# A two-layer graph network on one core: gathers released by the sums of the group that used the buffer, own terms inside the edge stages, setup and node stages rewritten without loops

## The chip, the core and the metric

The kernel runs on one core of one Trainium2 chip. A core has five engines with queues of their own: PE (TensorE, matrix products), DVE (VectorE), ACT (ScalarE), POOL (GpSimd) and SP (SyncE, which here only starts DMAs). They work side by side and wait for one another through semaphores. The metric is the time of one execution of the program in microseconds, taken on the device.

## What is computed

6250 nodes with 160 floats each (64 scalars and 32 vectors of three components), 200000 edges sorted by destination, and two layers. Each takes a message per edge, sums the messages by destination, mixes them and adds them to the node, and normalizes the row. Layer 0, shortened:

```python
xs, xv = node_input[:, :64], node_input[:, 64:].reshape(n, 32, 3)
s_s, s_v = xs * attr @ Ws_sc_a + ..., ...            # own terms, attributes a and c
x1s, x1v = l1a_s + l1c_s, l1a_v + l1c_v              # what the edges gather
weight = silu(edge_length_embedded @ W_fc1) @ W_fc2  # 192 weights per edge
gs, gv = x1s[edge_src], x1v[edge_src]
mid0a = w0 * gs * e_s
mid0b = w3 * (einsum('euc,ec->eu', gv, e_v) / sqrt(3))
mid1a = w1[:, :, None] * gs[:, :, None] * e_v[:, None, :]
mid1b = w2[:, :, None] * gv * e_s[:, :, None]
agg = segment_sum(edge_feat, edge_dst) / sqrt(16)
o = ((agg @ Ws_l2) @ Ws_l3) ...
x = layernorm(x + C_S * s + C_X * o)
```

Layer 1 is alike, with 224 weights per edge from 64 features, a fifth message (`w5 * cross(ev, e1) / sqrt(2)`), and at the end `silu` of 64 scalars and a `sigmoid` gate on the 32 vectors: `x = layernorm(x + gated)`.

## The kernel before

Nodes are padded to 6400, in 50 tiles of 128. Edges are cut into G = 392 groups of 512 (four tiles of 128 edges), four groups to a body, 98 bodies. There are five stages, each a block of its own with a barrier of all engines between: `setup_phase`, `edge_phase` of layer 0, `layer0_nodes_phase`, `edge_phase` of layer 1, `layer1_nodes_phase`.

**Setup** computes for each tile of nodes the row that edges will gather, and stores it to `table0` in DRAM. PE does two products a tile (L243 with 96 rows of x, L244 with 64), ACT scales one half (L221), DVE adds the other (L277), and SP stores. Ahead of the tiles PE multiplies the l2 and l3 matrices (L233, 16 products), and DVE finds each group's lowest and highest destination (L252 converts to float, L254, L255) and later a running sum of how many windows a group needs beyond the first (the scan, L298, L299). POOL loads x and clears `sums` (L206), the array of 128 features by nodes in SBUF in which both layers add up.

**Edge stage.** For each group:

- POOL gathers 512 rows from `table{L}`, in four instructions of 128 rows (L415). It has four row buffers, one per group of a body. A group's gathers wait for `index_in` and for `msg_done` of the group that had the buffer, so for the end of DVE's messages.
- PE computes the hidden layer (L450), ACT its silu (L431), PE the edge weights (L461).
- DVE builds `match` (one where the edge's destination is column n of a window of 40 nodes, L537), ACT scales it with the components of the edge attribute (L438), 12 or 16 small instructions per group.
- DVE multiplies rows and weights to messages: L618, L624, L626, in layer 1 also L608, L609, L623, L629 for the cross product. The last one signals `msg_done`.
- PE sums (L470): products of messages (as weights, 64 or 32 columns wide, each width going to a part of PE's columns) with `match` (40 or 3 × 40 columns). Over a group they accumulate in one PSUM bank. Every float32 product appears in the trace as two records: 56 per group in layer 0, 72 in layer 1.
- DVE adds the window to `sums` (L557).

PE's order, written out, is hidden layer of group g, edge weights of g−1, sums of g−2. SP loads indices, edge inputs and attributes two groups at a time, each load waiting for the reader of the buffer.

**Node stages** run tile by tile in loops of ten: ACT copies a piece of `sums` into a staging tile (L741, L875), PE multiplies own terms (L768, L769) and aggregates (L771 to L773; layer 1 L908 to L911), DVE combines, takes mean and variance and normalizes; in layer 0 PE transposes the new row (L779, L780) and multiplies it for the next layer (L786 to L788), and SP stores the new x, the new table and the own terms of layer 1. POOL loads, and at the end of the stage clears `sums` (L717).

## Time and profile before

| what | us |
|---|---|
| median of 3 runs | 4455.87 (4447.93 to 4457.54) |
| the profiled execution | 4453.04 |
| its span, from the first to the last instruction | 4451.0 |
| PE busy | 4044.4 (91%) |
| POOL busy | 3054.0 (69%) |
| ACT busy | 2961.5 (67%) |
| DVE busy | 2847.8 (64%) |

The mean granted PE clock over the span is 0.976 of full speed. A row of the timeline reads: start and length in us, engine, line of the kernel, operation, what it writes <- what it reads, shape, how many of the like in a row; in brackets how long the engine had been idle before it and what ended that. "PEld" is PE's loading of weights, which overlaps its products. "issue" is idle time in which the engine waited for nothing that the profile shows. A share of busy time doesn't tell what bounds a stage: that is read from the stage's own rows, in the section behind the diff.

### The profile page before, as it was taken

Reading aid. Unit: us, or ns where it says so; the run is one execution under the profiler, and the core shown is the slowest. Engines: PE = TensorE matmul, PEld = TensorE weight load, DVE = VectorE, ACT = ScalarE, POOL = GpSimd, SP = SyncE. Lnnn points to the kernel's source line nnn. Section 1 sums busy time; section 2 is a strip of 40 time slices with the busy share of each in tenths; the row PEclk is TensorE's granted clock in tenths of the full one; section 3 lists DMA queues with packets and bytes.
Section 4 is the critical chain, followed back from the end, with each engine's and each line's share of the span. In section 5 each row is a group of like instructions: output and inputs, shape, how many; then the busy total and the mean of one; then the engine's idle time right before and its main releaser. Section 6 shows DMA issues by size and latency. Waiting matters only on the chain. (4 is left out here: it accounts for less than half of the span.)

```text
span 4451.0 us, 166762 instructions
## 1 busy us (share of the span) xinstructions
PE 4044.4 (91%) x58000; PEld 3053.2 (69%) x58001; DVE 2847.8 (64%) x7746; ACT 2961.5 (67%) x12216; POOL 3054.0 (69%) x3215
## 2 busy tenths in 40 slices
PE   7888888888888888888979999999999999999987
PEld 4677777777777777776756766666666666666666
DVE  4544444444444444444667888888888888888878
ACT  1566666666666666665337877777777777777753
POOL 2577777777777777776017777777777777777751
PEclk9999999999999999999889999999999999999995
DMA  4222222222222222223334444444444444444433
GB/s 107 71 72 73 72 72 72 72 73 73 72 73 73 72 72 72 72 73 68 104 98 129 121 120 120 122 121 120 121 121 121 121 121 121 122 121 121 121 100 94
DMA packets 356348, 430.11 MB, mean 97 GB/s; under 512 B 203298, under 2 KB 248648, under 8 KB 356112
## 3 DMA queue, kind: packets, MB, share of 16 engines
q0 software_dynamic: 156288, 329.79, 27.4%
q1 hardware_dynamic: 199618, 98.11, 8.2%
q10 hardware_dynamic: 400, 1.68, 0.1%
q8 instruction: 23, 0.38, 0.0%
q14 instruction: 19, 0.16, 0.0%
HBM read 405.56 MB, written 23.74 MB: 96 GB/s over the span
## 5 line engine op out<-in xcount | busy, mean ns | idle before, releaser
L415 POOL DMA_INDIRECT e_rows<-scratch_table,e_index x3136 | 2967.3, 946 | 1010.5 <-issue 926.2
L438 ACT ACTIVATE e_match<-e_match,e_attr 128x40 f32<-128x40 f32 x10976 | 2480.9, 315 | 176.3 <-DMA e_attr<-in_edge_attr 172.1
L470 PEld LDWEIGHTS e_sum<-e_match,e_msg 128*64 128x64 f32 (+1 forms) x50176 | 1714.0, 125 | 698.3 <-DVE e_msg L629 244.3
L470 PE MATMUL e_sum<-e_match,e_msg 128*64 128x40 f32 (+2 forms) x50176 | 1846.2, 223 | 247.5 <-DVE e_msg L626 194.6
L461 PE MATMUL e_w<-k_fc,e_hidden 100*128 100x192 f32 (+1 forms) x4704 | 1275.2, 407 | 0.0
L618 DVE TENSOR_TENSOR e_msg<-e_w,e_rows 128x512 f32<-128x512 f32 x784 | 537.8, 686 | 1008.1 <-DMA e_rows<-scratch_table,e_index 980.0
L461 PEld LDWEIGHTS e_w<-k_fc,e_hidden 100*128 100x128 f32 (+1 forms) x4704 | 833.0, 190 | 385.3 <-issue 364.8
L431 ACT ACTIVATE e_hidden<-e_h 100x512 f32<-100x512 f32 (+1 forms) x784 | 384.4, 490 | 925.9 <-PE e_h L450 921.2
L450 PE MATMUL e_h<-e_inputs,k_fc 128*100 128x512 f32 (+1 forms) x1568 | 708.6, 534 | 57.9 <-DMA e_inputs<-in_inputs 27.0
L608 DVE TENSOR_TENSOR e_misc<-e_misc,e_rows 128x384 f32<-128x384 f32 x392 | 221.8, 566 | 354.2 <-DMA e_rows<-scratch_table,e_index 354.1
L624 DVE TENSOR_TENSOR e_msg<-e_w,e_rows 128x384 f32<-128x384 f32 x784 | 428.1, 546 | 0.0
L626 DVE TENSOR_TENSOR e_msg<-e_w,e_rows 128x384 f32<-128x384 f32 x784 | 428.0, 546 | 0.0
L450 PEld LDWEIGHTS e_h<-e_inputs,k_fc 128*100 128x100 f32 (+1 forms) x1568 | 216.0, 177 | 115.8 <-issue 54.9
L537 DVE TENSOR_TENSOR e_match<-e_misc,e_dst_rel 128x160 f32<-128x160 f32 x788 | 248.0, 315 | 13.3 <-DMA e_dst_rel<-scratch_dst_rel 11.1
L557 DVE TENSOR_TENSOR sums<-sums,e_sum 128x120 f32 (+1 forms) x784 | 226.3, 289 | 18.5 <-PE e_sum L470 16.9
L609 DVE TENSOR_TENSOR e_cross_b<-e_misc,e_rows 128x384 f32<-128x384 f32 x392 | 214.3, 547 | 0.0
L623 DVE TENSOR_TENSOR e_msg<-e_misc,e_cross_b 128x384 f32<-128x384 f32 x392 | 214.1, 546 | 0.0
L629 DVE TENSOR_TENSOR e_msg<-e_w,e_msg 128x384 f32<-128x384 f32 x392 | 213.4, 544 | 0.0
L601 DVE TENSOR_TENSOR e_match<-e_misc,e_match 128x160 f32<-128x160 f32 x392 | 123.4, 315 | 0.3 <-DVE e_match L537 0.2
L712 POOL DMA_DIRECT2D m_xv<-in_xT_v x10 | 5.4, 540 | 153.9 <-DVE m_y L805 142.5
L588 DVE COPY e_misc<-e_attr 128x48 f32<-128x48 f32 x392 | 79.8, 203 | 18.3 <-issue 5.9
L741 ACT ACTIVATE m_staged<-sums 128x384 f32 (+1 forms) x50 | 26.0, 522 | 97.1 <-PE m_agg L773 80.8
(122 smaller groups left out, 1454.0 us busy)
## 6 DMA issues: line engine op xcount, KB each, us to landing
e_rows<-scratch_table,e_index POOLq DMA_INDIRECT x3136
e_inputs<-in_inputs SPq DMA_DIRECT2D x196, 256.0 KB
e_attr<-in_edge_attr SPq DMA_DIRECT2D x392, 24.0 KB, 1.7
e_inputs<-in_inputs SPq DMA_DIRECT2D x196, 40.0 KB
e_index<-in_src SPq DMA_DIRECT2D x392, 4.0 KB
scratch_self<-m_h SPq DMA_DIRECT2D x10, 480.0 KB, 4.5
f_self<-scratch_self POOLq DMA_DIRECT2D x10, 480.0 KB, 5.0
m_xrow<-in_x POOLq DMA_DIRECT2D x10, 400.0 KB, 5.0
```

What stands on the lines that cost most here:

```text
L415: pool.indirect_dma_start(out=rows[j][:, t, :], out_offset=None, in_=table_dram, in_offset=bass.IndirectOffsetOnAxis(ap=index[q][:, c:c + ...
L431: nc.scalar.activation(hidden[j % 2][:, :], ps_h[0:layer.hid, 0:layer.group_cols], ACT.Silu, scale=layer.silu_scale).then_inc(silu_done, 1)
L438: last = nc.scalar.activation(match[j][:, t, c, :], match[j][:, t, 4, :], ACT.Copy, scale=attr[q][:, e0 + t, e:e + 1])
L450: nc.tensor.matmul(ps_h[0:layer.hid, 0:n], w[f"fc1_{L}"][:, :], inputs[j // 2][:, (j % 2) * n:(j % 2) * n + n], start=True, stop=True).the ...
L461: last = nc.tensor.matmul(ps_w[j % 2][:, c0:c0 + n], hidden[j % 2][:, u * P:(u + 1) * P], w[f"fc2_{L}"][:, :], start=True, stop=True)
L470: return nc.tensor.matmul(out[rows, c0:c0 + n, :], m[:, t, f:f + rows.stop - rows.start], m5[:, t, which:which + n, :], start=(first and t ...
L537: return nc.vector.tensor_tensor(into[:, :, 4, :], iota_t, rel_of(g).unsqueeze(2).broadcast_to([P, TPG, WIN]), ALU.is_equal)
L557: nc.vector.tensor_tensor(at, at, window, ALU.add).then_inc(added, 1)
L608: nc.vector.tensor_tensor(comps(cross_a), e3(3), comps(r[:, :, 96:192]), ALU.mult)
L618: nc.vector.tensor_tensor(m[:, :, 0:128].rearrange("p t (k n) -> p t k n", k=2), wt[:, :, 0:128].rearrange("p t (k n) -> p t k n", k=2), r ...
L624: nc.vector.tensor_tensor(comps(m[:, :, 128:224]), w_v(128), comps(r[:, :, 64:160]), ALU.mult)
L626: last = nc.vector.tensor_tensor(comps(m[:, :, 224:320]), w_v(160), comps(r[:, :, 64:160]), ALU.mult)
```

## The change

Nothing of what is computed changes, but nearly every stage is rewritten.

**Gathers.** A row buffer is now released by `sum_done`, the end of PE's sums for the group that used it, not by `msg_done`. The first four groups of a stage wait for nothing: the index buffers are four instead of two, are kept over stages, and are first filled in setup. POOL's loop covers two bodies per turn. A gathered row has 160 floats in both layers. On POOL's queue, in layer 0's loop, before (a row per run of like instructions; `DMA` is a gather):

```order
L415 DMA e0_rows0<-scratch_table0,e0_index0 128x160 [waits e0_msg_done0,e0_index_in0,e0_prepared]
L415 DMA e0_rows0<-scratch_table0,e0_index0 128x160 x3
L415 DMA e0_rows1<-scratch_table0,e0_index0 128x160 [waits e0_msg_done1,e0_index_in0,e0_prepared]
L415 DMA e0_rows1<-scratch_table0,e0_index0 128x160 x3
L415 DMA e0_rows2<-scratch_table0,e0_index1 128x160 [waits e0_msg_done2,e0_index_in1,e0_prepared]
```

and now, at the start of the stage and the head of the loop:

```order
L542 DMA e0_rows3<-scratch_table0,k_index3 128x160 x3
L549 UNCONDITIONAL_BRANCH
L549 ISA
L553 ISA
L542 DMA e0_rows0<-scratch_table0,k_index0 128x160 [waits e0_sum_done,e0_index_in0,e0_prepared]
L542 DMA e0_rows0<-scratch_table0,k_index0 128x160 x3
L542 DMA e0_rows1<-scratch_table0,k_index0 128x160 [waits e0_sum_done,e0_index_in0,e0_prepared]
```

The runs of four gathers stay; the semaphore that each run waits for is another one, and the wait compares it with a sum held in registers.

**Sums.** All products are 32 columns wide, dealt to the four quarters of PE's columns in turn: ten per tile in layer 0 and twelve in layer 1, so 80 and 96 records per group. Layer 1's cross product is no longer formed by DVE; its two halves are two more messages with their own `match` component, the second with negated weights. PE's queue, layer 0, one group's sums before:

```order
L470 MATMUL e_sum<-e_match,e_msg 64x120 [waits e0_scaled,e0_msg_done0]
L470 MATMUL e_sum<-e_match,e_msg 64x40 x2
L470 MATMUL e_sum<-e_match,e_msg 64x120
L470 MATMUL e_sum<-e_match,e_msg 64x40 x2
L470 MATMUL e_sum<-e_match,e_msg 64x120
L470 MATMUL e_sum<-e_match,e_msg 64x40 x2
L470 MATMUL e_sum<-e_match,e_msg 64x120
L470 MATMUL e_sum<-e_match,e_msg 64x40 x2
L470 MATMUL e_sum<-e_match,e_msg 32x40 x16
```

and now, in a group that also carries own terms (`e_xb` is a tile of x, transposed):

```order
L607 MATMUL e_sum<-e_match,e_msg 32x120
L607 MATMUL e_sum<-e_match,e_msg 32x40 x8
L607 MATMUL e_sum<-e_match,e_msg 32x120 x2
L607 MATMUL e_sum<-e_match,e_msg 32x40 x8
L607 MATMUL e_sum<-e_match,e_msg 32x120 x2
L607 MATMUL e_sum<-e_match,e_msg 32x40 x8
L607 MATMUL e_sum<-e_match,e_msg 32x120 x2
L607 MATMUL e_sum<-e_match,e_msg 32x40 x8
L637 MATMUL e_sum<-k_node_v,e_xb 128x2x96 [waits e0_base_in]
L638 MATMUL e_sum<-k_node_s,e_xb 128x2x64
```

The 64-wide products are gone, the two products of own terms stand behind the group's sums and ahead of the signal `sum_done`.

**Own terms** of tile i are computed in body i of the edge stage, i < 50, two PE products and two DVE operations, into `nodes`, which stays in SBUF (`base`, `node_terms`); SP loads the tile and in layer 1 stores the scaled own terms.

**Layer 1's edge weights** take four products of 64 rows and 256 columns instead of two of 128 rows and 480.

**Setup.** Tiles are written out one by one. x comes in large pieces on SP's and ACT's queues; all products have 128 rows (DVE clears the 32 rows that pad x). Ten products of the identity with itself stand in front, the l matrices' fold (four products) behind tile 44, the groups' minimum and maximum on DVE at tiles 13 and 17 without the conversion, and the scan is replaced by one PE product. POOL clears `sums` in seven pieces and ACT does an eighth.

**Node stages** are written out tile by tile. PE reads `sums` itself as weights, with no staging copy. In layer 0 the row isn't normalized before it is transposed; the next layer's weights are centred in setup, and the scaling by 1/deviation is applied behind. PE's queue in the middle of layer 0's stage, before:

```order
L768 MATMUL m_self<-k_node_v,m_xv 128x2x96 [waits m_y_ready,m_stage_done]
L769 MATMUL m_self<-k_node_s,m_xs 128x2x64
L771 MATMUL m_agg<-k_out,m_staged 128x320
L772 MATMUL m_agg<-k_out,m_staged 128x2x64
L773 MATMUL m_agg<-k_out,m_staged 128x2x96
L779 MATMUL m_tr<-k_ident,m_x_0 96x128 [waits m_trs_copied,m_x1_ready]
L780 MATMUL m_tr<-k_ident,m_x_0 64x128
L786 MATMUL m_next<-k_node_v,m_x1Tv 128x2x96 [waits m_h1_ready,m_trs_copied]
L787 MATMUL m_next<-k_node_s,m_x1Ts 128x64
L788 MATMUL m_next<-k_node_s,m_x1Ts 128x96
```

and now:

```order
L933 MATMUL m_agg<-k_out,sums 128x2x64 [waits m_y_done]
L934 MATMUL m_agg<-k_out,sums 128x2x64
L935 MATMUL m_agg<-k_out,sums 128x2x32
L937 MATMUL m_agg<-k_out,sums 128x2x64
L943 MATMUL m_tr<-k_ident,nodes 128x128 [waits m_tr_copied,m_momented]
L944 MATMUL m_tr<-k_ident,nodes 128x128
L950 MATMUL m_next<-k_node_v,m_yT 128x96 [waits m_h_ready,m_tr_copied]
L951 MATMUL m_next<-k_node_s,m_yT 128x64
```

Own terms have left the tile, and half of the next layer's product (its own terms) too. POOL clears `sums` tile by tile behind the products (L865). In layer 1's stage the own terms come in four loads, ACT normalizes in six batches, and 11 stores follow.

The core of the diff:

```diff
@@ edge_phase, POOL @@
-            def gather(count, j):
-                q = j // 2
-                pool.wait_ge(prepared, 1)
-                pool.wait_ge(index_in[q], count)
-                pool.wait_ge(msg_done[j], count)
+            def gather(count, summed, parity, j):
+                k = 2 * parity + j // 2
+                if not isinstance(count, int):
+                    pool.wait_ge(prepared, 1)
+                    pool.wait_ge(index_in[k], count)
+                    pool.wait_ge(sum_done, summed[GPB * parity + j])
+                elif parity:
+                    pool.wait_ge(sum_done, j + 1)
...
-            for j in range(GPB):
-                gather(16, j)
-            with pool.Fori(32, 16 * BODIES + 16, 16) as count:
-                for j in range(GPB):
-                    gather(count, j)
+            for parity in range(2):
+                for j in range(GPB):
+                    gather(0, None, parity, j)
+            with pool.Fori(1, BODIES // 2) as pair:
+                count = 32 * pair
+                summed = [2 * GPB * pair + (o - GPB + 1) for o in range(2 * GPB)]
+                for value in (count, *summed):
+                    pool.compute_val(value)
+                for parity in range(2):
+                    for j in range(GPB):
+                        gather(count, summed, parity, j)
@@ edge_phase, PE @@
-                    c0, n = u * layer.tiles_per_product * WPITCH, w[f"fc2_{L}"].shape[1]
-                    last = nc.tensor.matmul(ps_w[j % 2][:, c0:c0 + n], hidden[j % 2][:, u * P:(u + 1) * P], w[f"fc2_{L}"][:, :],
-                                            start=True, stop=True)
+                    for h in range(layer.tiles_per_product):
+                        c0, k = (u + 2 * h) * WPITCH, fc2.shape[0] // layer.tiles_per_product
+                        last = nc.tensor.matmul(ps_w[j % 2][:, c0:c0 + n], hidden[j % 2][k * h:k * h + k, u * P:(u + 1) * P],
+                                                fc2[k * h:k * h + k, :], start=True, stop=True)
...
-            def window_sums(j, m5):
+            def tile_sums(out, m, m5, opens, closes):
+
+                def product(g, c0, f, which, n=1, first=False, end=False):
+                    return nc.tensor.matmul(out[32 * g:32 * g + 32, c0:c0 + n, :], m[:, f:f + 32],
+                                            m5[:, which:which + n, :], start=first and opens, stop=end and closes)
+                product(0, 0, 64, 0, n=3, first=True)
+                product(1, 0, 96, 0, n=3, first=True)
+                product(2, 0, 128, 3, first=True)
+                product(3, 3, 224, 0, first=True)
+                if L == 0:
+                    product(2, 1, 160, 3)
+                    product(3, 3, 256, 1)
+                    product(0, 3, 0, 3, end=True)
+                    product(1, 3, 32, 3, end=True)
+                    product(2, 2, 192, 3, end=True)
+                    return product(3, 3, 288, 2, end=True)
...
+                if with_base:
+                    last = base(i)
+                last.then_inc(sum_done, 1)
```

## Rows read from the trace of the kernel before

**Rows 1.** Page of the profile: the span, and the gathers' line with its idle time.
```profile
span 4451.0 us, 166762 instructions
L415 POOL DMA_INDIRECT e_rows<-scratch_table,e_index x3136 | 2967.3, 946 | 1010.5 <-issue 926.2
```

**Rows 2.** Timeline: start us, us, engine, line, what, [idle before it <-releaser]. Gathers of both layers.
```profile
138.02 1.02 POOL L415 DMA_INDIRECT e_rows<-scratch_table,e_index  x1 [31.21 <-DVE e_misc L528]
...
993.74 0.95 POOL L415 DMA_INDIRECT e_rows<-scratch_table,e_index  x1 [0.30 <-issue]
...
1002.49 0.95 POOL L415 DMA_INDIRECT e_rows<-scratch_table,e_index  x1 [0.30 <-issue]
1003.75 0.95 POOL L415 DMA_INDIRECT e_rows<-scratch_table,e_index  x1 [0.30 <-issue]
...
2098.14 0.95 POOL L415 DMA_INDIRECT e_rows<-scratch_table,e_index  x1 [0.31 <-issue]
...
2338.41 1.01 POOL L415 DMA_INDIRECT e_rows<-scratch_table,e_index  x1 [24.40 <-DMA e_index<-in_src]
...
4298.60 0.95 POOL L415 DMA_INDIRECT e_rows<-scratch_table,e_index  x1 [0.30 <-issue]
```

**Rows 3.** Timeline of PE: one group of layer 0.
```profile
999.78 1.47 PE L461 MATMUL e_w<-k_fc,e_hidden 100*128 100x192 f32 x8
1001.71 2.12 PE L470 MATMUL e_sum<-e_match,e_msg 128*64 128x120 f32 x56 [0.46 <-DVE e_msg L626]
1003.75 1.10 PE L450 MATMUL e_h<-e_inputs,k_fc 128*100 128x512 f32 x2
```

**Rows 4.** One line's instructions: L470 on PE in two stretches of that group.
```profile
L470 PE MATMUL e_sum<-e_match,e_msg x24: 229/229/317, 1001.7 to 1002.6; 128*64 128x40 f32 x16, 128*64 128x120 f32 x8
L470 PE MATMUL e_sum<-e_match,e_msg x34: 202/202/229, 1002.5 to 1003.6; 128*32 128x40 f32 x32, 128*64 128x40 f32 x2
```

**Rows 5.** Timeline of layer 1: one group on PE; the last group's sums and addition.
```profile
3001.72 0.70 PE L450 MATMUL e_h<-e_inputs,k_fc 128*128 128x256 f32 x2
3002.26 1.77 PE L461 MATMUL e_w<-k_fc,e_hidden 128*128 128x480 f32 x4
...
4306.88 0.54 DVE L629 TENSOR_TENSOR e_msg<-e_w,e_msg 128x384 f32<-128x384 f32 x1
...
4307.48 4.10 PE L470 MATMUL e_sum<-e_match,e_msg 128*64 128x120 f32 x72 [4.07 <-DVE e_msg L629]
4311.78 0.32 DVE L557 TENSOR_TENSOR sums<-sums,e_sum 128x160 f32 x1 [4.13 <-PE e_sum L470]
```

**Rows 6.** Timeline of setup.
```profile
4.34 21.59 POOL L206 MEMSET sums<- 128x25760 f32 x1
7.34 19.68 DVE L252 TENSOR_SCALAR dst_by_group_f<-dst_by_group 98x2048 f32<-98x2048 int32 x1 [7.20 <-DMA dst_by_group<-in_dst_by_group]
...
20.00 7.09 PE L233 MATMUL ps_out<-s_l 96*128 96x32 f32 x32 [20.00 <-DMA s_l<-in_l]
...
41.96 1.01 PE L243 MATMUL s_psn<-k_node_v,s_xv 96*128 96x192 f32 x2 [11.74 <-DVE h L277]
42.89 0.50 PEld L244 LDWEIGHTS s_psn<-k_node_s,s_xs 64*128 64x128 f32 x2 [0.44 <-issue]
...
43.62 0.50 PEld L243 LDWEIGHTS s_psn<-k_node_v,s_xv 96*128 96x128 f32 x2 [0.22 <-issue]
...
122.39 0.38 DVE L277 SCALAR_TENSOR_TENSOR h<-s_psn,k_attr,part_a 128x160 f32<-128x160 f32 x1 [1.28 <-ACT part_a L221]
```

**Rows 7.** Timeline: the first stage of nodes, what precedes and ends it.
```profile
2109.21 0.28 DVE L557 TENSOR_TENSOR sums<-sums,e_sum 128x120 f32 x1 [3.75 <-PE e_sum L470]
...
2331.89 0.50 SPq L732 DMA_DIRECT2D scratch_self<-m_h  x1
```

**Rows 8.** Table of stretches: busy us (x) of PE, PEld, DVE, ACT, POOL, PEclk, DMA share, GB/s.
```profile
2120.00:2290.00 170.00, 163.78 (x767) 120.69 (x767) 115.41 (x401) 64.03 (x211) 15.96 (x24) 0.88 0.37 102
4320.00:4433.00 113.00, 95.16 (x384) 85.77 (x384) 94.49 (x447) 44.67 (x147) 13.92 (x16) 0.59 0.22 66
```

1274 lines of the change are left out of this document (715 added, 559 removed).

## The prediction, made before the changed kernel was run

> **What bounds the kernel now.** First the page: POOL's gathers are 3136 instructions, 2967.3 us busy, and the idle time before them is 926.2 us of "issue", time in which POOL waited for nothing that the profile shows [rows 1]. 926.2 over 3136 gathers is 0.30 us each, and the timeline has that 0.30 before every gather of the steady state: starts are 0.95 + 0.30 = 1.25 us apart [rows 2]. Then the ends of the two rows of gathers: layer 0 runs from 138.02 to 2098.14 + 0.95 = 2099.09, layer 1 from 2338.41 to 4298.60 + 0.95 = 4299.55 [rows 2]. Both are 1961.1 us for 1568 gathers, 1.251 each, though a row has 160 floats in the one and 224 in the other. So in 3922 of the 4451 us POOL issues gathers without a stop, and neither the release of a row buffer nor the bytes set the pace. Last what lies around them: setup 138.0; from layer 0's last gather to its last addition 2109.49 − 2099.09 = 10.4 [rows 2, 7]; the nodes' stage from there to layer 1's first gather 228.9; the same tail in layer 1 4312.10 − 4299.55 = 12.5 [rows 2, 5]; the last stage 4451.0 − 4312.1 = 138.9 [rows 1, 5]. These 528.8 us are all that the change can shorten, unless it changes the pace of POOL.
>
> **The edge stages.** The same 3136 gathers are issued, each still 128 rows. The release moves from the messages to the sums of the group that used the buffer. With four buffers a group's gathers start 4 × 5.0 = 20 us before the buffer is wanted again. The group whose sums run from 1001.71 to 1003.75 [rows 3] had its first gather at 993.74 [rows 2], the eighth before 1003.75: 10.0 us, so the new wait has some 10 us to spare. The worst cases are the last groups, with PE at slow clock: first gather 3.75 us before the last, sums over at 2109.21 and 4311.78 [rows 5, 7], that is 14.8 and 16.9 us, still under 20. The messages are queued on DVE and the sums on PE, in group order in both versions; who waits if the sums were late is POOL alone, with all later gathers behind it. I count the release at nothing, and what hides it is this slack. The register arithmetic of the new wait runs on POOL's queue at 49 loop heads where 97 were; the old heads cost nothing visible [rows 1, 2], and I take nothing.
>
> PE must stay under 5.0 us per group. In layer 0 it runs the hidden layer from 1003.75 to 1004.69 (the next start), 0.94; edge weights, eight records of 192 columns, about 1.30; sums 2.04 (1001.71 to 1003.75) [rows 3], together 4.3. The sums go from 56 records to 80 with 32-column weights, in layer 1 from 72 to 96. The 32-wide part of the old sums shows what such records cost: 32 of them start between 1002.8 and 1003.6, 26 ns each [rows 4] (the row's window also catches two of the 64-wide kind), though 24 of the 32 go to one group of PE's columns, so groups run beside each other. At 26 ns the new sums take 80 × 0.026 = 2.1 and 96 × 0.026 = 2.5 us. PE in layer 0: 0.94 + 1.30 + 2.1 = 4.3. In layer 1: hidden 0.54, edge weights 1.70 before (four records of 480 columns [rows 5]), less after (eight of 256), 2.5: at most 4.7. Below 5.0 both times. Own terms add two products every fourth group in the first 50 bodies, 4 records of at most 192 columns at 0.16 = 0.65 us, or 0.16 per group, and two DVE operations; DVE loses the two cross products and gains nothing else. So the gathers stay at 1961.1 each. In layer 1 the last group's messages lose two of seven operations, about 1.0 us of the 12.5; the last sums took 4.10 for 72 records at slow clock [rows 5] and change little. Tails: 9.3 and 10.5. At the start of a stage PE is slow and the pipeline fills; the first buffer's release may come up to 6 us late, I take 2 each.
>
> **Setup.** PE waited for the l matrices until 20.00, then for DVE until 41.96 [rows 6]; DVE's 19.68 us conversion lay beside POOL's 21.59 us clearing of `sums` [rows 6]. Both are gone: small loads come first, the fold goes behind tile 44, and the minimum reads the integers directly in the middle of the tiles. Then tiles come every 43.62 − 41.96 = 1.66 us, of which 0.44 + 0.22 is PE idle ahead of a weight load that changes the number of rows (96, 64); the new matrices all have 128 rows. I take 1.07 per tile, between 1.00 (1.66 less 0.66) and 1.14. If PE ran at its full clock it were half. These are slow-clock records: two of 192 columns take about twice the 0.16 each of [rows 3]. DVE's first input landed at 7.34 [rows 6]; PE starts at 6 to 7. So 6.5 + 53.5 = 60, and 4 for the last scaling, store and the barrier: first gather at **64**, against 138. Ends: 52 (some tiles at full clock) and 80 (PE's idle stays).
>
> **Layer 0's nodes.** The old tile cost: 401 DVE instructions in 170 us at nine a tile are 44.6 tiles, 3.81 us each, at a mean clock of 0.88 [rows 8]; 228.9 − 50 × 3.81 leaves 38 for start and end, with POOL's clearing of 19320 columns at the end, by [rows 6] 21.59 × 19320/25760 = 16.2. The new tile has no staging copy, no own terms, no loads: 14 PE records, 1472 columns; at 0.16 per 192 columns 1.23 us, or 1.51 if every record costs 128; at half clock 2.5 to 3.0. DVE has four operations, 4 × 115.41/401 = 1.15, and ACT about as much. Which clock PE gets is the unknown; I take 2.0 per tile, 100 us. POOL's clearing is now one piece per tile, 0.43 us (21.59 × 512/25760), beside DVE. If each stopped DVE as the one in [rows 6] did, DVE would be at 1.15 + 0.43 = 1.6, still under 2.0. Around the tiles 18 remain: 38 less 16.2, and less some 4 for the loads and clearings before the first gather. **118**, ends 100 (1.6 per tile, which is DVE so held up) and 165 (2.9, PE at half clock, and 20 around).
>
> The Trainium skill (SBUF — State Buffer, "Who interferes with whom") says that DVE in a 2-port mode and GpSimd lock each other out for the whole instruction, and that a DVE instruction with at most one SBUF input outside those modes isn't touched. [Rows 6] agree with the first half: 19.68 us beside 21.59. The new tile's two products-and-additions read PSUM and one SBUF operand, and the statistics read one. By the page DVE stays at 1.15, and the low end would be PE's 1.5 per tile, 93.
>
> **Layer 1's nodes.** 447 DVE instructions in 113 us, nine a tile, are 49.7 tiles, 2.27 us each, clock 0.59 [rows 8]; 138.9 − 50 × 2.27 = 25. New: five DVE operations, 5 × 94.49/447 = 1.06, up to 1.4 as the short ones are those that go; PE eight records, 896 columns, 0.75 fast and 1.5 slow. At 0.59 I take 1.6 per tile, 80 us. The final scaling is spread over the stage instead of standing at its end, 25 becomes 18. **98**, ends 84 (DVE's 1.3 per tile and 19) and 112 (1.8 and 22).
>
> **Sum.** 64 + 1961.1 + 2 + 9.3 + 118 + 1961.1 + 2 + 10.5 + 98 = 4226.0 of span. Before, the profiled run was 4453.04 for a span of 4451.0, and the median is 4455.87, 2.8 above that run: 4226.0 + 2.0 + 2.8 = 4230.8. I say **4230**, 5.1% less.
>
> **Rivals.**
> A. PE stays slow in all unrolled stages: setup 80, nodes 165 and 112, starts 6 each, 4226 + 16 + 47 + 14 + 8 = 4311 of span, **4316**. For it: the clock of 0.59 in the last stage; against: 0.88 in the other. The opposite end, all at full clock, 52 + 100 + 84 in place of 64 + 118 + 98, gives **4186**.
> B. The new products don't overlap. Then a 32-wide record of 40 columns costs 36 ns (24 in about 0.86 us on one group) and one of 120 three times that, 0.108: a tile in layer 0 has 4 × 0.108 + 16 × 0.036 = 1.0 us, the sums 4.0, PE 0.94 + 1.30 + 4.0 = 6.25. Layer 1: 4 × 0.108 + 20 × 0.036 = 1.15, sums 4.6, PE with 0.54 and 1.0 around them 6.15. Every group loses 1.2 us, 784 × 1.2 = 940, **5170**, slower than before. It decides from PE's 5.0 us on; to eat the 225 us gained, groups must come 0.29 us later, which is sums of about 3.05 in layer 0 with the like in layer 1. Against it: 32 records in 0.8 us. If instead the mean cost per record of the old sums held (2.04/56 = 36 ns), layer 0's sums take 2.9, PE 5.15, and only 392 × 0.15 = 60 is lost: **4290**.
> C. The release by sums, or the arithmetic of its wait, slows POOL. 0.1 us per group would be 78 us, **4308**; it would decide only if that work can't run ahead of the gathers, and the 0.30 before each gather doesn't change at the old loop heads.
> D. The change of release or of row length quickens the gathers. The two layers' equal 1.251 speaks against it. Each 1% would be 39 us.
>
> **How the numbers follow.** Forecast as worked out, 0.68, within 4186 to 4280. A 0.12, B in full 0.04, B's mild form 0.06, C 0.07, D 0.03. The range takes in the ends of the stages, B's mild form and part of C, A: 4186 to 4300. Faster by over 0.2% (about what a measurement of this kernel can tell from no change) 0.95; within it 0.01; slower 0.04.
>
> **What would show it.** Gathers still 1.25 us apart with 0.30 of "issue", no idle of POOL on `sum_done` except near a stage's start; first gather near 64, stages of 118 and 98 between a last addition and what follows; the sums 2.1 and 2.5 us long, PE's start of sums still right behind the messages. It would be wrong if PE rather than POOL ran without a pause in the edge stages, if POOL waited on PE in the steady state, or if the tiles of the unrolled stages came more than 2.5 us apart.

## The result, and the profile after

The changed kernel took **4156.67 us** (4154.38 to 4158.72), the one before in the same rounds 4456.7 (4447.93 to 4457.57): a ratio of 0.9331, 95% interval 0.9315 to 0.9347, so 6.7% less. I had forecast 4230 and a range of 4186 to 4300. The direction was right, the gain was 300 us and not 227, and the time lies below the range.

The page of the changed kernel, its span, its PE clock in 40 slices and the line of the gathers:

```profile
span 4157.0 us, 230556 instructions
PEclk9999999999999999999999999999999999999998
L542 POOL DMA_INDIRECT e_rows<-scratch_table,k_index x3136 | 2972.7, 948 | 997.4 <-issue 900.6
```

The clock row has no slice below 8, the last one included, where the kernel before ended on a 5. The gathers are as in [rows 1]: 948 ns each and 0.3 of "issue".

The timeline of POOL, the four gathers at the ends of the stages, and DVE's last additions (start, length, engine, line):

```profile
51.49 1.10 POOL L542 DMA_INDIRECT e_rows<-scratch_table,k_index  x1 [30.05 <-POOLq L108]
...
2014.82 0.95 POOL L542 DMA_INDIRECT e_rows<-scratch_table,k_index  x1 [0.30 <-issue]
...
2024.71 0.32 DVE L736 TENSOR_TENSOR sums<-sums,e_sum 128x160 f32 x1 [2.42 <-PE e_sum L607]
...
2112.83 0.95 POOL L542 DMA_INDIRECT e_rows<-scratch_table,k_index  x1 [11.60 <-POOLq L832]
...
4076.11 0.95 POOL L542 DMA_INDIRECT e_rows<-scratch_table,k_index  x1 [0.30 <-issue]
...
4088.05 0.32 DVE L736 TENSOR_TENSOR sums<-sums,e_sum 128x160 f32 x1 [3.60 <-PE e_sum L607]
```

These answer to [rows 2, 5, 7] and give the stages (last gather's end = its start + 0.95):

| stretch | before | forecast | after | after − forecast |
|---|---|---|---|---|
| start to first gather | 138.0 | 64 | 51.5 | −12.5 |
| layer 0's gathers | 1961.1 | 1963.1 | 1964.3 | +1.2 |
| last gather to last addition | 10.4 | 9.3 | 9.3 | 0.0 |
| layer 0's nodes, to the next gather | 228.9 | 118 | 87.8 | −30.2 |
| layer 1's gathers | 1961.1 | 1963.1 | 1964.2 | +1.1 |
| last gather to last addition | 12.5 | 10.5 | 11.3 | +0.8 |
| last stage | 138.9 | 98 | 68.6 | −29.4 |

All of the gain, 294 us of span, lies outside the gathers, as the first part of the prediction said. Nearly all of the error lies in the three stages that are now written out. The table of stretches for them (busy us and count of PE, PEld, DVE, ACT, POOL, then PEclk, DMA share, GB/s), to be held against [rows 8]:

```profile
8.00:20.00 12.00, 9.74 (x69) 9.47 (x68) 5.39 (x16) 8.87 (x19) 12.00 (x5) 1.00 1.04 267
20.00:31.00 11.00, 6.09 (x24) 5.98 (x23) 7.29 (x11) 2.21 (x7) 1.44 (x1) 0.69 1.05 308
2042.00:2100.00 58.00, 58.00 (x524) 58.00 (x522) 37.79 (x165) 30.70 (x83) 19.43 (x37) 1.00 0.40 131
4093.00:4140.00 47.00, 43.80 (x383) 42.98 (x381) 45.21 (x218) 35.44 (x129) 0.00 (x0) 1.00 0.45 136
```

PEclk is 1.00 in three of the four, the upper of PE's two levels (2.4 GHz), where the old node stages had means of 0.88 and 0.59. The fourth, 20 to 31 us, is the middle of setup: PE stood 4.91 us for DVE, which waited for the destinations, and the next five tiles came 1.07 us apart at the lower level (1.2 GHz). In layer 0's stage PE is busy for 58.00 of 58 us: 524 records at 14 a tile are 37.4 tiles, 1.55 us each. In the last stage 383 records at eight a tile are 47.9 tiles in 47 us, 0.98 each, and DVE with 45.21 of 47 us sets that.

One group's sums of each layer on PE, beside [rows 3, 5], and their count in layer 0:

```profile
1001.92 1.54 PE L607 MATMUL e_sum<-e_match,e_msg 128*32 128x120 f32 x80 [0.99 <-DVE e_msg L805]
...
3004.18 2.16 PE L607 MATMUL e_sum<-e_match,e_msg 128*32 128x120 f32 x128 [1.61 <-DVE e_msg L808]
L607 PE MATMUL e_sum<-e_match,e_msg x80: 196/207/290, 1001.9 to 1003.3; 128*32 128x40 f32 x64, 128*32 128x120 f32 x16
```

80 records start between 1001.9 and 1003.3, 17 ns apart. In layer 1 there are 128 records to a group (the page counts 81536 in 392 groups of each layer, 80 + 128). I had counted 96, from twelve products per tile; the kernel has sixteen. They take 2.16 us, 15 ns from start to start. Starts so close, against 26 ns where 24 of 32 records went to one quarter of PE's columns [rows 4], say that the quarters work side by side; which of them sets the time isn't shown.

### The profile page after: what moved, and what is told of

It is laid out like the page before. It is cut to its first block and busy times, and to the rows that moved or that the text cites. A ratio compares the mean times of both kernels' runs of the same rounds, so it can differ in the third digit from the quotient of the medians.

```text
span 4157.0 us, 230556 instructions
## 1 busy us (share of the span) xinstructions
PE 3299.3 (79%) x91130; PEld 2543.6 (61%) x91131; DVE 2369.4 (57%) x6461; ACT 2898.8 (70%) x12105; POOL 3019.7 (73%) x3206
## 3 DMA queue, kind: packets, MB, share of 16 engines
q1 hardware_dynamic: 209936, 122.14, 10.4%
## 5 line engine op out<-in xcount | busy, mean ns | idle before, releaser
L542 POOL DMA_INDIRECT e_rows<-scratch_table,k_index x3136 | 2972.7, 948 | 997.4 <-issue 900.6
L607 PE MATMUL e_sum<-e_match,e_msg 128*32 128x40 f32 (+1 forms) x81536 | 1438.0, 215 | 707.1 <-DVE e_msg L805 362.5
L607 PEld LDWEIGHTS e_sum<-e_match,e_msg 128*32 128x32 f32 x81536 | 1294.1, 111 | 1024.4 <-DVE e_msg L808 396.7
L600 PE MATMUL e_w<-k_fc,e_hidden 100*128 100x192 f32 (+1 forms) x6272 | 1025.5, 365 | 1.0 <-issue 1.0
L803 DVE TENSOR_TENSOR e_msg<-e_w,e_rows 128x384 f32<-128x384 f32 x784 | 429.0, 547 | 0.0
L805 DVE TENSOR_TENSOR e_msg<-e_w,e_rows 128x384 f32<-128x384 f32 x784 | 429.0, 547 | 0.0
L702 DVE TENSOR_TENSOR e_match<-e_misc,k_dst_rel 128x160 f32<-128x160 f32 x788 | 248.8, 316 | 2.1 <-issue 0.7
L736 DVE TENSOR_TENSOR sums<-sums,e_sum 128x160 f32 x784 | 242.9, 310 | 9.3 <-PE e_sum L607 8.5
L807 DVE TENSOR_TENSOR e_msg<-e_w,e_rows 128x384 f32<-128x384 f32 x392 | 214.2, 547 | 0.0
L808 DVE TENSOR_TENSOR e_msg<-e_w,e_rows 128x384 f32<-128x384 f32 x392 | 213.9, 546 | 0.0
L779 DVE COPY e_e_kept<-e_attr 128x48 f32<-128x48 f32 x392 | 81.7, 209 | 6.5 <-issue 3.6
L865 POOL MEMSET sums<- 128x512 f32 (+1 forms) x50 | 26.4, 528 | 59.1 <-PE m_agg L937 59.1
L903 ACT ACTIVATE m_yT<-m_tr 128x256 f32<-128x256 f32 x50 | 19.2, 386 | 47.9 <-PE m_tr L944 47.9
L778 DVE COPY e_misc<-e_attr 128x48 f32<-128x48 f32 x196 | 40.5, 207 | 10.3 <-DMA e_attr<-in_edge_attr 1.2
```

What stands on the lines that cost most here:

```text
L542: pool.indirect_dma_start(out=rows[j][:, t, :], out_offset=None, in_=table_dram, in_offset=bass.IndirectOffsetOnAxis(ap=index[k][:, c:c + ...
L600: last = nc.tensor.matmul(ps_w[j % 2][:, c0:c0 + n], hidden[j % 2][k * h:k * h + k, u * P:(u + 1) * P], fc2[k * h:k * h + k, :], start=Tru ...
L607: return nc.tensor.matmul(out[32 * g:32 * g + 32, c0:c0 + n, :], m[:, f:f + 32], m5[:, which:which + n, :], start=first and opens, stop=en ...
L702: return nc.vector.tensor_tensor(into[:, :, 4, :], iota_t, rel_of(g).unsqueeze(2).broadcast_to([P, TPG, WIN]), ALU.is_equal)
L736: nc.vector.tensor_tensor(at, at, window, ALU.add).then_inc(added, 1)
L803: nc.vector.tensor_tensor(comps(m[:, :, 128:224]), w_v(128), comps(r[:, :, 64:160]), ALU.mult)
```

## The experiments

My theory after the result: the release is worth nothing, and most of the gain comes from PE having its upper level in the three written-out stages, because all products there have 128 rows and PE no longer stands between tiles. The first half held where the kernel before takes 4450 us. Of the second half the runs and the old trace leave little: the level explains most of what I had forecast too high, and only the smaller part of the gain. The rivals: those stages are shorter through the steps that they no longer do, whatever PE's level; and the edge stages gain from the release. The seventeen runs are told by the question that they answer, and each expectation says what its theories make of it. The first four were made on a chip on which the kernel before took 7562 us instead of 4455 (seven runs, 7535 to 7574). Their setups and node stages are as elsewhere, their edge stages are not, so only the former are used, and what the latter show is told at the end. All others ran where the kernel before took 4450 to 4454.

### The control

> The changed kernel once more, as a control on the chip of its neighbours in this group. If the chip is like that of the first measurement: 0.933 of the kernel before, 4155 to 4160 us. If it is like that of the first four experiments, where the kernel before took 7562 us and PE stood still between single records while gathers ran: about 6500, 0.86 of before.

Measured: 4148.2 us, 0.9321 of before (0.9305 to 0.9336), stages 48.1, 1959.9, 96.6 (last gather of layer 0 to first of layer 1), 1960.9, 79.1 (last gather to the end). The first measured chip had 51.5, 1964.3, 97.1, 1964.2, 79.9. So chips differ by 4 us in an edge stage, and by 3 in setup, where DVE waits for the destinations to arrive; below I compare with the control.

### What set PE's level in setup

The edit, two products of setup back to 96 and 64 rows:

```diff
-                nc.tensor.matmul(out[:, :, S:D], x_v[:, k * P:(k + 1) * P], w["node_v0"][:, 0:192], start=True, stop=True)
-                nc.tensor.matmul(out[:, :, 0:S], x_s[:, k // 2 * P:(k // 2 + 1) * P], w["node_s0"][:, P * (k % 2):P * (k % 2) + P],
+                nc.tensor.matmul(out[:, :, S:D], x_v[0:V3, k * P:(k + 1) * P], w["node_v0"][0:V3, 0:192], start=True, stop=True)
+                h = S * (k % 2)
+                nc.tensor.matmul(out[:, :, 0:S], x_s[h:h + S, k // 2 * P:(k // 2 + 1) * P], w["node_s0"][h:h + S, P * (k % 2):P * (k % 2) + P],
```

> The changed kernel with setup's two products per tile back at 96 and 64 rows; nothing else differs. Theory 1 (the alternation of row counts is what kept PE at its slow level in the old setup, by the idle before each weight load): tiles come about 1.4 to 1.7 us apart instead of 0.55, the records last as in the old setup (about 1.0 and 0.8 us a pair), first gather near 51 + 45 = 96 us (85 to 105). Theory 2 (the alternation costs only its idle, the clock follows from other things): 0.2 to 0.35 us more per tile at full clock, first gather at 62 to 70.

> The same kernel as the first run with 96 and 64 rows, for its setup on a chip where the kernel before takes 4450 us. Theory 1 (changing row counts hold PE at its slow level): first gather again near 95, 45 us later than the control's 48 to 51, and the whole 4190 to 4200. Theory 2: 62 to 70.

Both runs had their first gather at 95.0, and the second took 4196.19 in all. The second run's timeline, and its table for most of setup:

```profile
60.56 0.50 PEld L288 LDWEIGHTS s_psn<-k_node_v,s_xv 96*128 96x128 f32 x2 [0.22 <-issue]
60.56 1.01 PE L288 MATMUL s_psn<-k_node_v,s_xv 96*128 96x192 f32 x2
...
61.50 0.50 PEld L290 LDWEIGHTS s_psn<-k_node_s,s_xs 64*128 64x128 f32 x2 [0.44 <-issue]
61.50 0.79 PE L290 MATMUL s_psn<-k_node_s,s_xs 64*128 64x128 f32 x2
62.22 0.50 PEld L288 LDWEIGHTS s_psn<-k_node_v,s_xv 96*128 96x128 f32 x2 [0.22 <-issue]
12.00:90.00 78.00, 78.00 (x196) 48.20 (x195) 23.53 (x66) 19.61 (x55) 9.42 (x4) 0.50 0.37 106
95.00 1.10 POOL L543 DMA_INDIRECT e_rows<-scratch_table,k_index  x1 [73.58 <-POOLq L108]
```

The pairs last 1.01 and 0.79, tiles come 1.66 apart, and 0.44 and 0.22 of idle stand before the weights: to the hundredth the old setup [rows 6]. Here the clock is on record, 0.50, the lower level (1.2 GHz), from 12 to 90 us. So products of 96 and 64 rows in turn bring the old setup's tile and its lower level back, and 128 rows in all of them were worth 47 us (95.0 against 48.1), of which by estimate only 50 × 0.33 = 16 are the idle itself at full clock (half of the 0.66 measured at the lower level). Theory 1 holds for what the edit does. What in it acts, the change from product to product, the smaller number of rows or the idle before each weight load, no run tells apart. The change alone doesn't hold PE down everywhere: in the old layer 0's node stage products of 96, 64 and 128 rows follow one another at the upper level (rows further down).

The same part put alone into the kernel before (x and weights padded to 128 rows by DVE):

> The kernel before with one part of the change: setup's products padded to 128 rows. Theory 1: tiles come at full clock, at ACT's and DVE's pace of 0.5 to 0.8 us, and the first gather moves from 138 to 95 (90 to 105). Theory 2: only the idle of 0.66 per tile goes, 48 tiles save 28 to 32 us, first gather at 107 to 110.

```profile
80.83 0.59 PE L245 MATMUL s_psn<-k_node_v,s_xv 128*128 128x192 f32 x2 [0.57 <-DVE h L285]
...
81.48 0.49 PE L245 MATMUL s_psn<-k_node_v,s_xv 128*128 128x192 f32 x2
81.81 0.38 PE L246 MATMUL s_psn<-k_node_s,s_xs 128*128 128x128 f32 x2
...
66.00:96.00 30.00, 18.25 (x108) 15.58 (x107) 13.44 (x38) 11.01 (x28) 4.17 (x8) 1.00 0.53 137
```

The first gather came at 108.4 against 138.0. I had set this up so that 107 to 110 would speak for theory 2, and it falls there. But the rows show pairs of 0.49 and 0.38, which is the upper level; the tiles are held up by something else, since PE waits for x and for DVE between them (18.25 us busy in the 30 from 66 to 96). The time of the first gather couldn't tell the two apart; the record durations do. The rows show one thing more: PE stood 0.57 us in every second tile here, was busy 61% of the time, and kept a clock of 1.00.

> The changed kernel without the ten identity products ahead of the tiles. If they are what brings PE to full clock by 7 us, the first tiles run at 1.07 us each and the first gather comes 2 to 6 us later (53 to 57). If the tiles themselves do it as soon, within 1 us of 51.5.

First gather at 48.45, no later than with them (50.8 in the run beside it). At first PE did run at the lower level, until 15.1 us, but it then waited less for DVE, which was itself waiting for the destinations. The ten products buy nothing here.

### What set PE's level in the node stages

In the last stage, PE's wait before a tile's products moved from eight tiles back to one:

```diff
-                at_least(pe, pre_ready, n - BANKS + 1)
+                at_least(pe, pre_ready, n)
```

> Last stage only: PE's products of tile n wait until DVE has read tile n-1, as if there were one PSUM bank instead of eight. Theory 1 (the slow level that I carried over from the old last stage, 0.59 of full clock, came from PE standing still between tiles, and goes once PE is fed without a stop): PE stands still 0.5 us per tile and falls back to its slow level for most of the stage; tiles 1.9 to 2.2 us, the stage 40 to 60 us longer. Theory 2 (the waits don't lower it): 0.9 for the products and 0.45 for the reading, 1.35 per tile against 1.1, 10 to 18 us longer, at full clock.

The whole took 4231.8, and from the last gather to the end 154.4 against 79.1, 75 more.

```profile
4182.00 0.80 PE L1056 MATMUL f_ps<-k_out,sums 128*128 128x128 f32 x2 [0.51 <-DVE f_pre L1100]
...
4184.58 0.80 PE L1056 MATMUL f_ps<-k_out,sums 128*128 128x128 f32 x2 [0.51 <-DVE f_pre L1100]
4093.00:4230.00 137.00, 100.23 (x387) 85.79 (x386) 57.41 (x261) 52.21 (x163) 0.00 (x0) 0.50 0.18 56
```

Tiles are 2.58 us apart, with 0.51 of standing still in each, and the clock is 0.50 over the whole stretch. The changed kernel's tile is 0.98, so the wait cost 1.6 us per tile: 0.5 is the stand, the larger part is PE's level. This is theory 1, and it was dearer than I had said (40 to 60). What kept the level low isn't settled by it: in the setup above stands of 0.57 us went with the upper level. The two stretches differ in what came first. Here PE stood 3.23 us for DVE before the second tile and was at the lower level from then on; there it was at the upper level when the stands began.

The same in layer 0's stage, one tile earlier:

```diff
-                at_least(pe, y_done, n - 2)
+                at_least(pe, y_done, n - 1)
```

> Layer 0's node stage: PE's aggregation of tile n waits for DVE's second addition of tile n-2, one tile earlier than in the changed kernel. PE has 14 records, 1.56 us, per tile; the chain aggregation, two DVE additions and their signals is about 1.4. If this makes PE stand still for 0.2 us or more per tile and that is enough for the slow level, tiles take 2.5 to 3.0 us and the stage 50 to 70 us more. If PE's other products (0.66 us) fill the wait, tiles stay at 1.56 and nothing changes. I hold the second for likelier, 2 to 1.

```profile
2020.00:2054.00 34.00, 27.83 (x149) 24.48 (x139) 10.40 (x42) 4.28 (x9) 5.76 (x11) 0.50 0.07 20
2041.21 0.80 PE L933 MATMUL m_agg<-k_out,sums 128*128 128x128 f32 x2 [0.34 <-DVE nodes L972]
...
2056.00:2110.00 54.00, 49.57 (x395) 45.73 (x394) 28.42 (x123) 22.88 (x62) 14.68 (x28) 1.00 0.30 100
2061.32 0.49 PE L933 MATMUL m_agg<-k_out,sums 128*128 128x128 f32 x2 [0.16 <-DVE nodes L972]
```

The stage took 31.7 us more (128.3 against 96.6). I had held it for likelier that nothing would change. Until 2054.6 the level is the lower one, 33 us from the last addition, where the changed kernel and the control took 6 and 5 us. In that time tiles come 2.84 apart and PE stands in each, 0.77 us in the first ones and 0.34 later. The level rises in the first tile in which PE doesn't stand, since by then its other products fill the wait. Behind it tiles come 1.92 apart instead of 1.55, with stands of 0.16, and the upper level stays. So stands of 0.34 us and more went with a rise that came some 28 us late; stands of 0.16 didn't undo it.

What the level was worth in the gain is read from the old trace, where layer 0's stage has both levels. Here one old tile at the upper one, with the table of the stretch around it, and the table of the old last stage at the lower one:

```profile
2148.69 0.59 PE L768 MATMUL m_self<-k_node_v,m_xv 96*128 96x192 f32 x2
2149.21 0.49 PE L769 MATMUL m_self<-k_node_s,m_xs 64*128 64x128 f32 x2
...
2152.07 0.59 PE L768 MATMUL m_self<-k_node_v,m_xv 96*128 96x192 f32 x2
...
2140.00:2180.00 40.00, 39.78 (x215) 29.62 (x214) 29.40 (x104) 17.58 (x60) 4.12 (x7) 1.00 0.46 124
4346.00:4420.00 74.00, 69.52 (x253) 62.43 (x252) 60.73 (x285) 28.46 (x96) 10.44 (x12) 0.50 0.24 74
```

At the upper level the old tile of layer 0 took 3.38 us, against 3.81 in the mean and 1.55 now. So by estimate 0.43 us per tile, some 20 us of the 141 that the stage lost, is the level, and 1.83 per tile, some 90 us, is work that left the tile; the rest lies around the tiles. In the old last stage, 0.50 from 4346 to 4420, DVE was busy 1.90 us of each tile (94.49 us in 49.7 tiles [rows 8]) and would have set the pace at any level; so by estimate the level is at most 0.37 of the 1.29 us by which the tile shrank, 18 us. PE was busy 69.52 of those 74 us, all products had 128 rows, and it was at the lower level all the same; why isn't shown. With the 47 us of setup, in which the idle before weight loads is included, at most some 90 of the 294 us come from the level and the rows, and the rival (steps that are no longer done) has the larger part.

### POOL's clearing

```diff
-            for n in range(NT):
-                pool.wait_ge(agg_mm, n + 1)
-                nc.gpsimd.memset(sums[:, :, n * P:(n + 1) * P if n < NT - 1 else SUMW], 0.0)
+            pool.wait_ge(agg_mm, NT)
+            nc.gpsimd.memset(sums[:, :, :], 0.0)
```

> POOL clears the sums in one piece after the last aggregation of layer 0's node stage, as the old kernel did, not tile by tile. The piece takes 21.5 us, and beside it lie about 7 us of the last tiles and stores and the barrier behind. From layer 0's last gather to layer 1's first 97 becomes 110 to 116, all else the same: 14 to 19 us more in all. In my sum this was a term of 16.

```profile
2093.59 21.57 POOL L864 MEMSET sums<- 128x25760 f32 x1 [84.02 <-PE m_agg L936]
```

9.9 us more between the gathers (106.5 against 96.6), less than expected: 12 us of the 21.6 lie beside the last tiles, the stores and the barrier. The term of 16 in my sum, for a clearing of 16.2 us in the old stage, was too large: here one of 21.57 us was worth 10.

### The release

The changed kernel with the old condition, and three values held in registers for the waits instead of nine:

```diff
-                    pool.wait_ge(sum_done, summed[GPB * parity + j])
+                    pool.wait_ge(msg_done[j], summed[parity])
```

> The changed kernel with row buffers released by the messages as before. My theory (the release is hidden by 8 to 10 us of slack): the same time, within 3 us, gathers 1.25 us apart, edge stages of 1961 to 1965 us each. Rival (the release by sums does cost or gain): a change of more than 0.2%, 9 us. The 1.5 us by which 1568 gathers took longer than in the kernel before would go if the register arithmetic of the new wait caused it.

> Row buffers released by the messages, all else as changed, beside the control. Theory 1 (the release is hidden by slack where POOL sets the pace): within 0.2% of the control on a chip where POOL sets the pace. Theory 2 (the release by sums keeps gathers from running far ahead while PE is starved of its instructions): where PE sets the pace, the messages' release is slower by 10 to 20%, as 7808 against 6500 us in the first four; and then POOL stands in long waits (5 to 16 us) and runs of gathers with PE's records 0.7 us apart beside them.

On the chip of the control: 4147.07 (4145.36 to 4148.06) against 4148.2 (4146.29 to 4149.14). The table of waits of POOL, columns waited for, us in total, times, longest, first of this run, then of the control:

```profile
POOL e_rows L542 <- issue: 948.9, 3116, 0.3
```

```profile
POOL e_rows L542 <- issue: 860.9, 2825, 0.7
POOL e_rows L542 <- PE e_sum L607: 93.9, 305, 1.3
```

Both are 0.3 us per gather, 949 in 3116 gathers here, 861 + 94 in 3130 there; the release is only another name for the same gap. Theory 1 holds: the edit that gives the change its name is worth nothing on such a chip, within 0.1%.

To see the slack itself, the wait was made two groups tighter (`sum_done` of group g − 2 instead of g − 4):

> Row buffers released only by the sums of the group two before, instead of four before: the wait is made tight on purpose. A group's first gather then can't start before the sums of the group two earlier are done, 10.1 us after that one's first gather in layer 0 and 12 to 12.6 in layer 1. Where POOL set the pace at 5.01 us per group, the pace becomes about 5.1 in layer 0 (+30 to 60 us over 392 groups) and 5.8 to 6.2 in layer 1 (+300 to 450 us). If the whole is slower by less than 100 us, the time from gather to sums isn't what I read.

```profile
POOL e_rows L542 <- PE e_sum L607: 612.0, 299, 6.6
```

4883.69 us; layer 0's gathers took 2113.5 (+154), layer 1's 2542.3 (+581). The direction is as expected, the size is larger: groups of 5.39 and 6.49 us give 10.8 and 13.0 us from a group's first gather to the next that may start behind its sums. From four groups back, at 20 us, that leaves 9 and 7 to spare. But in this run PE's clock fell as well (0.88 over layer 1's edges, by the table of stretches), which lengthens the time that it measures. The changed kernel's own rows, the first gather of the two groups whose sums are shown behind the result, give it without that:

```profile
993.75 0.94 POOL L542 DMA_INDIRECT e_rows<-scratch_table,k_index  x1 [0.31 <-PE e_sum L607]
...
2994.66 0.95 POOL L542 DMA_INDIRECT e_rows<-scratch_table,k_index  x1 [0.30 <-issue]
```

The sums end at 1003.46 and 3006.34, 9.7 and 11.7 us later, so 10 and 8 us are to spare. The slack of 10 that I gave is right in layer 0 and 2 too large in layer 1.

### What would bound the edge stages next

```diff
-                for t in range(TPG):
+                for t in range(TPG // 2):
```

> Of the four gathers of a group only two are issued; the rows of the other two edge tiles are zeros, so the output leaves half of the messages out. It shows what bounds the edge stages once POOL doesn't: POOL would need 2.5 us per group. In layer 0 PE needs about 0.94 + 1.30 + 1.6 = 3.9, ACT 3.3, DVE 2.7; in layer 1 ACT 4.0, PE 3.5, DVE 3.4. So groups at 3.9 to 4.1 in both layers, 392 times 1.0 less in each, about 3350 us in all (3250 to 3500). If the stages hardly shorten, POOL wasn't the bound.

3268.03 us; the edge stages took 1517 and 1521, 3.87 and 3.88 us per group.

```profile
POOL e_rows L542 <- PE e_sum L607: 1099.8, 676, 8.3
...
1000.36 1.30 PE L607 MATMUL e_sum<-e_match,e_msg 128*32 128x120 f32 x80
...
3000.68 2.08 PE L607 MATMUL e_sum<-e_match,e_msg 128*32 128x120 f32 x128
...
200.00:1500.00 1300.00, 1248.23 (x30406) 962.50 (x30405) 877.92 (x2436) 1080.74 (x4370) 634.91 (x673) 1.00 0.23 58
1800.00:3000.00 1200.00, 1178.47 (x42948) 919.83 (x42946) 991.00 (x2410) 1176.03 (x5268) 585.20 (x621) 1.00 0.32 88
```

Now POOL waits 1100 us for PE's sums, so POOL was the bound. The next one is PE in layer 0 (busy 1248 of 1300 us). In layer 1 PE (1178 of 1200) and ACT (1176) are both full, and the run doesn't tell which of them sets the 3.9. Some 21% of the whole (3268 against 4148) is all that faster gathers could bring.

### The sums' widths

Layer 0's four products on the lower half of the columns made two of 64 columns, in the order of the changed kernel:

```diff
-                product(0, 0, 64, 0, n=3, first=True)
-                product(1, 0, 96, 0, n=3, first=True)
+                product(0, 0, 64, 0, n=3, first=True, wide=64)
...
-                    product(0, 3, 0, 3, end=True)
-                    product(1, 3, 32, 3, end=True)
+                    product(0, 3, 0, 3, end=True, wide=64)
```

> Layer 0's sums with two of the ten products per tile 64 columns wide in place of four of 32 (64 records a group instead of 80). If the quarters of PE's columns work side by side, the busiest quarter sets the time and it hardly changes: 1.7 us for the sums before, 1.6 to 1.8 now. If records are served one after another, it falls by a fifth, to 1.35. The time of the whole doesn't change (within 3 us), since POOL sets the pace.

4779.11 us, **slower than the kernel before**, layer 0's gathers 2582.9 instead of 1959.9. Neither alternative had said this.

```profile
1000.41 4.27 PE L607 MATMUL e_sum<-e_match,e_msg 128*64 128x120 f32 x64
1000.76 0.89 PEld L607 LDWEIGHTS e_sum<-e_match,e_msg 128*32 128x32 f32 x16 [0.16 <-issue]
...
1001.81 0.89 PEld L607 LDWEIGHTS e_sum<-e_match,e_msg 128*32 128x32 f32 x16 [0.16 <-issue]
```

A group's sums take 4.27 us for 64 records. The rows of weight loads, 16 to a tile (four 64-wide, twelve 32-wide, put together under the shape of the first), come every 1.05 us, so each tile takes 1.05. In a tile the widths stand in the order 64, 32, 64, 32, so there are 15 changes in a group, not the eight that the next expectation counts. With the same products sorted, all 64-wide ones of a group first:

> Layer 0's sums with the same 64- and 32-wide products as in the run with mixed widths (64 records per group, 4.3 us there), but all 64-wide products of a group first and then all 32-wide, one change of width in a group instead of eight. Theory 1 (each change between widths makes PE wait until the array is empty): 1.6 to 2.1 us, the whole at 4145 to 4155 us, like the control. Theory 2 (64-wide products are dear in themselves): the sums stay above 3 us and the whole near 4780.

```profile
1003.67 2.46 PE L607 MATMUL e_sum<-e_match,e_msg 128*64 128x120 f32 x64
```

4153.12 us, within 0.12% of the control. The sums take 2.46 us. So the change of width is dear: 14 changes fewer save 1.8 us per group, 0.13 each. The time lies between the two theories (1.6 to 2.1, over 3): sorted in this way, 64 records still take 0.9 us more than the changed kernel's 80 of 32 columns (1.54). Whether that is the price of 64 columns, or comes from the order, which puts first all of the work on one half of the columns and then all on the other, no run tells. The kernel before had its products sorted in this way [rows 4]. The Trainium skill (TensorEngine Tiling (Array Packing), "Key Properties") says that tiles work independently and that switching the tile mode drains the array. The two runs agree with the second half as far as its cost goes, 4.27 against 2.46 us for the same products; the draining itself stands in no row.

### Own terms

> The changed kernel without layer 0's own terms: the two PE products, the two DVE operations and the load of x transposed are left out of the first 50 bodies, so the output leaves them out as well. If they are hidden (PE has over 1 us to spare per group, DVE 2): layer 0's gathers take 1959 to 1962 us as in the control, the whole within 0.2% of it. If they delay the sums and through them the gathers: 5 to 30 us less.

4149.59 us, layer 0's gathers 1960.4 against the control's 1959.9 (this run on another chip, where the kernel before took 4452 us). They are hidden.

### Two tries at a faster kernel

> The groups' minimum and maximum are taken on DVE behind tiles 25 and 27 instead of 13 and 17, so that DVE doesn't wait for the destinations while PE waits for DVE. The 5.1 us idle of PE and the slow clock of 24 to 31 us after it should go: first gather at 43 to 46 us instead of 51.5, the rest unchanged, so 5 to 8 us less in all (0.1 to 0.2%).

4149.12 (4147.93 to 4149.81), 0.9323 of before (0.9307 to 0.9338): no gain, first gather at 50.4 against 48.1. On this chip the destinations arrived earlier, and the two reductions of 2.3 us now stood in the middle of tiles that flowed.

> A try at a faster version: in the last stage DVE bounds the tiles (five operations, about 1.2 us); the residual's addition (0.32) goes to POOL, which is idle there. If POOL's addition takes under 1 us and doesn't hold DVE up, tiles take 1.0 instead of 1.2 and the stage is 6 to 10 us shorter, 0.2% in all. If POOL and DVE hold each other up, or POOL needs over 1.2 us, it is longer by 5 to 30 us.

4145.3 (4144.03 to 4148.23), 0.9304 of before (0.9289 to 0.932) against the control's 0.9321; the intervals overlap.

```profile
4111.16 0.50 POOL L1056 TENSOR_TENSOR nodes<-nodes,f_post 128x160 f32<-128x160 f32 x1 [0.42 <-DVE f_post L1112]
...
4124.05 0.39 DVE L1107 SCALAR_TENSOR_TENSOR f_pre<-f_ps,k_attr,f_self 128x192 f32<-128x192 f32 x1
...
4124.83 0.39 DVE L1107 SCALAR_TENSOR_TENSOR f_pre<-f_ps,k_attr,f_self 128x192 f32<-128x192 f32 x1
```

POOL's addition takes 0.50 us, tiles can come 0.78 apart where DVE needed 1.02, and from the last gather to the end 73.1 us pass instead of 79.1. The stage is 6 us shorter, as expected; in the whole this can't be told from no change, though the median is the lowest of all versions.

### The other chip

The four runs on the chip where the kernel before took 7562 us: 7532 us for the kernel before with its setup padded to 128 rows, 6535 and 6500 with the release by sums, and 7808 with the release by messages (0.86 of before the two, 1.033 with an interval of 1.031 to 1.036 the last). The timeline of PE in the middle of the last one, while POOL issued gathers:

```profile
3003.41 0.36 PE L607 MATMUL e_sum<-e_match,e_msg 128*32 128x40 f32 x3 [1.21 <-issue]
...
3014.90 1.75 PE L607 MATMUL e_sum<-e_match,e_msg 128*32 128x120 f32 x80
```

Single records stand 0.7 us or more apart, with "issue" before them; at 3014.90, when POOL waited and issued nothing for 9.56 us, 80 records ran in 1.75 us. I read this so: on that chip gathers under way take something from PE that the profile doesn't name, PE becomes the bound, and a condition that lets POOL run further ahead makes it worse. It is argued from such stretches; no run tested it. Here the release by sums is worth some 17%, if other things are equal; I have the control only on the other chip, so the size rests on two neighbours that differ in setup alone. What PE is kept from isn't shown, and why one chip does this and not the others stays open.

## Why the prediction was off, point by point

- **The bound, right.** POOL's gathers set the pace in both versions; the edge stages stayed within 3.2 us, and only what lies around them changed. Half the gathers confirm it.
- **The release at nothing, right** where it was measured against the control (4147.07 and 4148.20). The slack of 10 us was 10 in layer 0 and 8 in layer 1, which I had bounded only by the tail's 16.9 us from gather to sums. The arithmetic of the wait costs nothing that can be seen. On the other chip the same term wasn't nothing (some 17%), and the prediction had no rival for that.
- **The sums, right in the verdict, wrong in the count.** I took 26 ns per record from [rows 4] and 96 records in layer 1. It is 128 records, at 15 ns. That the verdict held is partly luck, since the two errors worked against each other (2.5 us forecast, 2.1 to 2.2 measured). Had the records cost 26 ns, 128 would have taken 3.3 us, and PE 5.0 with hidden layer and weights: at the edge. The row that I used had 24 of its 32 records on one quarter of the columns and told more of that quarter's price than of four.
- **Setup, 64 forecast, 51.5 measured.** The step that failed is "I take 1.07 per tile". Taking away the 0.66 of idle from a tile of 1.66 left me with slow records; the run with 96 and 64 rows shows that the idle and the slow records come and go together. The tiles came 0.55 apart. That the low end, 52, fits is luck: with 0.55 for every tile my own sum would have been 6.5 + 27.5 + 4 = 38. The rest are terms that it didn't have: stands of PE of 1.67, 0.59 and 4.91 us, five tiles at the lower level behind the longest (2.6 us more), and the other products among the tiles.
- **Layer 0's nodes, 118 forecast, 87.8 measured.** The step that failed is the term "I take 2.0 per tile"; it was 1.55. At 1472 columns I had 1.23 and, with every record at 128, 1.51; the latter is the measured one within 0.04, at the upper level. I had mixed in a lower level that the old stage had in part. And even the lowest value that I worked out, 93 with 1.5 per tile, was 5 too high, because the 18 around the tiles are 10 (87.8 less 50 × 1.55). My end of 1.6, DVE held up by POOL's clearings, didn't come either: beside 19.43 us of POOL's work DVE was busy 37.79 us in 37.4 tiles, 1.01 each.
- **Layer 1's nodes, 98 forecast, 68.6 measured.** The step that failed is "At 0.59 I take 1.6 per tile", the same as above: 0.98 to 1.02 were measured, DVE's own pace, with PE at its upper level. My low bound of 1.3 came from DVE's 1.4 for five operations; their timeline shows 1.02, since an operation starts before the one ahead of it has ended in the records. 5 × 0.211 = 1.06 was the better of my own two numbers.
- **The range.** What I called the corner with all stages at full clock gave 4186, and I made it the end of the range. It wasn't at full clock by my own numbers (38, 93 and, with 1.06 per tile and 19 around them, 72 would have been), and all three stages ran at the upper level nearly throughout. The level that a stage had in the old kernel didn't carry over to a stage with other work.
- **The rivals.** A (slow everywhere) didn't come; the run with PE's wait moved to one tile back shows what it would have looked like in the last stage. B's mechanism, sums that don't overlap, was not there; its price was, in the run with mixed widths, where PE needed 6.6 us per group and the kernel lost to the one before. C fell on the chips where POOL sets the pace (no wait on `sum_done` beyond 0.3 in the first measurement, 1.3 in the control, with gathers as far apart as before). D fell (1.2527 us per gather against 1.2507, though layer 1's rows are 29% shorter).

## What to carry to other kernels

Don't price a rewritten stage by the old stage's clock: compute the new tile at the upper level first, find what then bounds it, and let the lower level be the rival, which here came with stands of 0.34 us and more in each tile, or with products of 96 and 64 rows in turn. Then ask, too, what the old tile cost at the upper level, or the clock gets credit for work that was simply taken out. Give products that follow one another the same number of rows and the same width, or sort them so that the width changes once: 47 us of setup and 1.8 us per group hung on it here. And where an engine that issues gathers sets the pace with a constant gap, leave its conditions alone and shorten what stands before and behind.
